# 66 slots instead of 68, quarter blocks, moved residuals and statistics, and inverse roots by Newton steps on VectorE

## The reference, cut to what matters

```
h = layernorm(x)                                # GNN: three layers
for i in range(3):
    m = h @ weight[i];  aggr = A^T @ m          # A = (adj != 0), per graph
    h = gru_cell(aggr, h)                       # sigmoid, sigmoid, tanh
x = x + h
xn = layernorm(x)                               # FFN: mixture of 8 experts
H = gelu(xn @ W1 + b1)                          # 128 -> 512
probs = softmax(H @ Wg + bg);  e = argmax(probs)
out = x + probs[e] * (H @ Wd[e] + bd[e])        # only the chosen expert counts
```

## Time and profile before

| | us |
|---|---|
| median of 3 runs (lowest, highest) | 468.53 (468.18, 469.12) |
| the profiled execution's own time | 469.11 |
| its span, first to last instruction | 467.4 |
| busy: PE, PEld (weight loads), DVE, ACT, POOL | 455.7, 377.4, 356.8, 323.0, 360.2 |
| indirect scatters to `sorted_rows` (line 580), busy | 63.9 in 64 instructions |
| indirect scatters to the output (line 591), busy | 35.6 in 36 and 31.8 in 32 |
| matmuls of the experts (line 858, 512 instructions) | 60.3 |

### The profile page before, as it was taken

One profiled execution on the slowest core, in us unless ns is written; L12 is line 12 of the kernel. 1 busy time (PEld: TensorE's weight loads), 2 busy tenths in 40 slices (PEclk: granted clock), 3 DMA queues, 4 the chain that ended last, 5 costly groups with the idle time before them and its releaser, 6 DMA issues.

```text
span 467.4 us, 10216 instructions
## 1 busy us (share of the span) xinstructions
PE 455.7 (97%) x3047; PEld 377.4 (81%) x3047; DVE 356.8 (76%) x1152; ACT 323.0 (69%) x576; POOL 360.2 (77%) x346
## 2 busy tenths in 40 slices
PE   8999999999999999999999999999999999999993
PEld 5777888888888888888888777777768989989993
DVE  5789878789888898887987889879778556556642
ACT  3776887777977769877788798888762553454340
POOL 4478997599978999889977757777777777277576
PEclk9999999999999999999999999999999999999998
DMA  7711455411234432111121111111452335454110
GB/s 199 211 42 51 137 145 148 136 45 45 58 86 109 132 100 80 52 45 47 51 58 51 52 47 40 59 53 58 134 142 79 112 115 167 126 155 118 38 52 28
DMA packets 69525, 42.10 MB, mean 90 GB/s; under 512 B 9548, under 2 KB 66128, under 8 KB 69472
## 3 DMA queue, kind: packets, MB, share of 16 engines
q1 hardware_dynamic: 64048, 32.33, 24.5%
q0 software_dynamic: 4224, 8.92, 5.5%
q10 hardware_dynamic: 1200, 0.20, 0.2%
HBM read 16.90 MB, written 9.84 MB: 57 GB/s over the span
## 4 chain that ended last, share of the span: by engine, by line
PE 90%; ACT 4%; DVE 3%; issue 1%; SPq 1%; POOL 1%; DMA 0%; POOLq 0%; DVEq 0%
PE bank L614 20%; PE bank L616 19%; PE bank L615 19%; PE bank L858 12%; PE bank L645 9%; PE bank L781 3%; ACT adj_i L1068 2%; PE bank L834 2%; PE bank L632 2%; PE bank L737 1%; PE bank L652 1%; PE bank L851 1%; SPq L372 1%; POOL out_dram L591 1%; DVE xrow L1277 0%
## 5 line engine op out<-in xcount | busy, mean ns | idle before, releaser
L1068 ACT ACTIVATE adj_i<-bank,b1c 128x512 f32<-128x512 f32 x132 | 88.6, 687 | 68.1 <-PE bank L616 67.4
L580 POOL DMA_INDIRECT sorted_rows<-xrow,pos x64 | 63.9, 999 | 24.4 <-issue 23.1
L477 POOL TENSOR_TENSOR diff<-hT,n_sb 128x512 f32<-128x512 f32 x48 | 67.3, 1403 | 17.4 <-ACT n_sb L955 17.3
L479 POOL TENSOR_TENSOR diff<-z_sb,diff 128x512 f32<-128x512 f32 x48 | 63.3, 1319 | 3.8
L858 PE MATMUL bank<-wd_sb,adj_i 128*128 x512 | 60.3, 275 | 0.0
L858 PEld LDWEIGHTS bank<-wd_sb,adj_i 128*128 128x128 f32 x512 | 59.0, 192 | 0.3
L614 PE MATMUL bank<-ag_hi,wf_hi 128*128 128x512 f32 x144 | 59.0, 410 | 0.1
L614 PE MATMUL bank<-hT_hi,w_hi 128*128 128x512 f32 x132 | 56.9, 431 | 1.1 <-ACT adj_i L1068 0.7
L615 PE MATMUL bank<-ag_lo,wf_hi 128*128 128x512 f32 x144 | 57.0, 396 | 0.0
L616 PE MATMUL bank<-ag_hi,wf_lo 128*128 128x512 f32 x144 | 56.9, 395 | 0.0
L614 PE MATMUL bank<-hT_hi,whh_hi 128*128 128x512 f32 x132 | 55.9, 424 | 0.0
(11 more groups left out here) (199 smaller groups left out, 1056.0 us busy)
## 6 DMA issues: line engine op xcount, KB each, us to landing
bands<-hT SPq DMA_DIRECT2D x192, 64.0 KB, 2.2
adj_i<-sorted_rows SPq DMA_DIRECT2D x64, 72.0 KB
xrow<-in_x_dram SPq DMA_DIRECT2D x16, 256.0 KB, 3.3
adj_i<-in_adj_dram SPq DMA_DIRECT2D x16, 256.0 KB, 3.8
wd_sb<-in_L_ffn_Wd_dram SPq DMA_DIRECT2D x8, 256.0 KB, 3.0
sorted_rows<-xrow,pos POOLq DMA_INDIRECT x64, 2.3
A<-wd_sb SPq DMA_DIRECT2D x4, 256.0 KB
hT<-wd_sb SPq DMA_DIRECT2D x4, 256.0 KB
```

The lines of the kernel that those rows point to most:

```text
L477: nc.gpsimd.tensor_tensor(diff[:, b, :], hT[:, g, :], n_sb[:, b, :], ALU.subtract).then_inc(diff_ok, 1)
L479: nc.gpsimd.tensor_tensor(diff[:, b, :], z_sb[:, g, :], diff[:, b, :], ALU.mult).then_inc(zd_ok, 1)
L580: nc.gpsimd.indirect_dma_start(out=sorted_rows, out_offset=bass.IndirectOffsetOnAxis(ap=pos[:, g, j:j + 1], axis=0), in_=xrow[:, g * GR + ...
L1068: nc.scalar.activation(HT[:, hb, k, 0:n], HB[k][:, 0:n], ACT.Gelu, bias=b1c[:, k:k + 1]).then_inc(done, 1)
```

## The change

The last six slots are now made of eight halves (four slots, all of slot group 15) and eight quarters of 32 rows (two slots, all of slot group 16). With quarters the worst case of padding is smaller, so SLOTS is 66. The number of slot groups stays 17. Sixteen copies of weights and biases take the place of eight. SP issues the first eight weight copies right behind `tab_ok` 2, before it waits for the scatters and before it loads slot group 6. The other eight and all biases go beside slot groups 6 to 13. The reads of table values lose their runtime bounds check.

The second table has three kinds of blocks, so `rest()` has more instructions and more stages that wait for each other.

In the gate, ScalarE takes `turned_high(1)` before the gelus of group 0 and does all four of these in a row. VectorE takes `turned_low(1)` earlier. The residual of the last unit moves to the end of gate step 4, and the last two groups' statistics from steps 4 and 5 to 5 and 6. The inverse roots of the last two groups are made on VectorE, by an integer first guess and three Newton steps, in gate steps 7 to 10. GpSimd's `pow` between the scatters goes.

TensorE waits for half of the gelus only, before the first two chunks of a slot group's hidden layer, and reads the table for slot group 0 ahead of them. `last_rows` has another order.

```diff
-    PIECE = P // 2
-    SLOTS = -(-((TOK + E * (PIECE - 1)) // PIECE) // PIECES)
+    HALF, QUARTER = P // 2, P // 4
+    HALVES = QUARTERS = E
+    COPIES = HALVES + QUARTERS
+    SLOTS = -(-((TOK + E * (QUARTER - 1)) // QUARTER) // (P // QUARTER))
-    WHOLE = (SGROUPS - 1) * GR
+    WHOLE = SLOTS - HALVES * HALF // P - QUARTERS * QUARTER // P
...
             _, found = nc.values_load_multi_w_load_instructions(row[0:1, at:at + count], engines=(engine,), min_val=0, max_val=top,
+                                                                skip_runtime_bounds_check_because="the table is bounded where it is made")
...
-        LATE_SCALES = 6
+        LATE_SCALES = 7
+        REFINED = 3
... (SP)
+            def load_weights(first, count):
+                at = entries(mybir.EngineType.SP, wd_tab, WHOLE + first, count, (E - 1) * KC * P)
+                for k in range(count):
+                    sp.dma_start(wd_last[first + k], wd_sb[:, bass.ds(at[k], KC * P)]).then_inc(e_wd, 16)
             sp.wait_ge(tab_ok, 2)
+            load_weights(0, HALVES)
             sp.wait_ge(g_late, (GROUPS - EARLY) * GR * 16)
             sp.wait_ge(pad_ok, (E + 1) * 16)
             for sg in range(EARLY_SG, SGROUPS):
                 load_rows(sg)
-                if sg == EARLY_SG + 2:
-                    last_at = (places(... wd_tab ...), places(... bd_tab ...))
-                if inside(sg - EARLY_SG - 2, GR * PIECES):
-                    load_last(sg - EARLY_SG - 2, *last_at)
+                if inside(sg - EARLY_SG, QUARTERS):
+                    load_weights(HALVES + sg - EARLY_SG, 1)
+                    load_biases((sg - EARLY_SG) * 2, 2)
... (GpSimd)
-                if s == LATE_SCALES + 1:
-                    which = slice(SCALED[LATE_BATCH] * GR, GROUPS * GR)
-                    pool.wait_ge(g_var_late, 1)
-                    nc.gpsimd.tensor_tensor(xrow[:, which, RSTD], xrow[:, which, RSTD],
-                                            half[...], ALU.pow).then_inc(g_rstd_late, 1)
... (TensorE)
             def rows_ready(sg):
-                hold(pe, e_h, sg * KC)
+                hold(pe, e_h, sg * KC - 2)
             def expert_pieces(sg, j, o):
                 for k in range(KC):
-                    for h in range(PIECES):
+                    for h in range(pieces(sg)):
             def step(s):
+                    if s == 1:
+                        at = weights_at(0)
                     rows_ready(s)
                     hidden(s % 2, (0, 1), e_w1)
-                    at = weights_at(s - 1)
+                    if s > 1:
+                        at = weights_at(s - 1)
+                    pe.wait_ge(e_h, s * KC)
                     hidden(s % 2, (2, 3), e_w1)
             def last_rows():
+                pe.wait_ge(e_h, two * KC)
+                pe.wait_ge(e_wd, 2 * COPIES * 16)
+                slot_alone(one, 0, None)
+                slot_alone(one, 1, None)
                 pe.wait_ge(e_xhi, two + 1)
                 pe.wait_ge(e_xlo, two + 1)
-                for j in range(GR):
-                    pe.wait_ge(e_h, one * KC + j + 1)
-                    hidden(two % 2, (j,), e_w1, cols(two))
-                    slot_alone(one, j, at_one)
+                hidden(two % 2, range(KC), e_w1, cols(two))
+                slot_alone(one, 2, None)
+                slot_alone(one, 3, None)
... (ScalarE, gate_step)
-                if s > 0 and inside(s + 1, GROUPS):
+                if inside(s + 1, GROUPS):
                     turned_high(s + 1)
-                    gelus(s % 2, s, (0, 1), g_w1, g_h)
+                    gelus(s % 2, s, (0, 1) if s else range(KC), g_w1, g_h)
                 if s == 0:
-                    turned_high(1)
                     new_state(UN - 1)
... (VectorE)
+            def late_guess():
                 dve.wait_ge(g_mv, GROUPS)
+                ts(late_var, late_var, EPS, None, ALU.add).then_inc(g_newton, 1)
+                ts(root_i[:], late_var.bitcast(i32), 1, None, ALU.arith_shift_right).then_inc(g_newton, 1)
+                ts(root_i[:], root_i[:], -1.0, float(0x5f3759df), ALU.mult, ALU.add).then_inc(g_newton, 1)
+            def late_refined(n):
+                tt(root_sq[:], root, root, ALU.mult).then_inc(g_newton, 1)
+                stt(root_sq[:], root_sq[:], -0.5, late_var, ALU.mult, ALU.mult).then_inc(g_newton, 1)
+                stt(late_var if n == REFINED else root, root_sq[:], 1.5, root, ALU.add, ALU.mult).then_inc(g_newton, 1)
+                if s == UN:
+                    turned_low(1)
-                turn, norm = inside(s + 1, GROUPS), ...
+                turn, norm = s > 0 and inside(s + 1, GROUPS), ...
-                measured = GROUPS - 6 + s
-                stat = s in (4, 5)
+                measured = GROUPS - 7 + s
+                stat = s in (5, 6)
                 if turn:
                     turned_low(s + 1)
+                if s == 4:
+                    state_rows(UN - 1)
+                    residual(UN - 1)
... (VectorE, rest: the added stages)
+                ts(until[:, 2 * E + 1:2 * E + 2], until[:, 2 * E:2 * E + 1], float(LATE_WHOLE + HALVES // 2), None, ALU.max)
+                dve.wait_ge(t_late, 16)
+                stt(until[:, 2 * E + 2:LISTS], many_cum[:, 2, :], 1.0 / 4, until[...], ALU.mult, ALU.add)
+                dve.wait_ge(t_late, 17)
```

More of the change, by code:

```diff
@@ L135, in build @@
         slot_i, slot = sb("slot_i", [P, 1], i32), sb("slot", [P, 1])
[L136 to L140, removed]
+        place, over, over_q = (sb(n, [P, 1]) for n in ("place", "over", "over_q"))
+        upward = sb("upward", [P, E])
+        ends_i, ends = sb("ends_i", [P, 3, E], i32), sb("ends", [P, 3, E])
+        many, many_cum = sb("many", [P, 3, E]), sb("many_cum", [P, 3, E])
+        many_t = sb("many_t", [P, 3, E, E])
         begins, offs = sb("begins", [P, LISTS + 1]), sb("offs", [P, LISTS + 1])
@@ L222, in places, with entries @@
         def places(engine, row, sg, top):
-            _, found = nc.values_load_multi_w_load_instructions(row[0:1, sg * GR:sg * GR + slots(sg) * pieces(sg)], engines=(engine,),
-                                                                min_val=0, max_val=top)
+            at, many_of = (first_piece(sg), slots(sg) * pieces(sg)) if pieces(sg) > 1 else (sg * GR, slots(sg))
+            return entries(engine, row, at, many_of, top)
+        def entries(engine, row, at, count, top):
+            _, found = nc.values_load_multi_w_load_instructions(row[0:1, at:at + count], engines=(engine,), min_val=0, max_val=top,
+                                                                skip_runtime_bounds_check_because="the table is bounded where it is made")
             return found
@@ L835, in turned_rows @@
                 last.then_inc(e_t, 1)
-            held = []
             def weights_at(sg):
@@ L1094, in gate_step @@
                         gate_rows(s + 3, 1)
-                if inside(s, GROUPS):
+                if s > 0 and inside(s, GROUPS):
                     gelus(s % 2, s, (2, 3), g_w1, g_h)
@@ L1541, in rest @@
+                stt(begins[:, E + 1:2 * E + 1], ends[:, 0, :], float(P), ecap[:], ALU.mult, ALU.add).then_inc(t_late, 1)
+                stt(begins[:, 2 * E + 2:LISTS], ends[:, 1, :], float(HALF), ecap[:], ALU.mult, ALU.add).then_inc(t_late, 1)
                 dve.wait_ge(t_late, 7)
+                tt(many_t[:], tri[:].unsqueeze(1).to_broadcast([P, 3, E, E]),
+                   many[:].unsqueeze(2).to_broadcast([P, 3, E, E]), ALU.mult).then_inc(t_late, 1)
+                dve.wait_ge(t_late, 10)
@@ L1560, in rest @@
+                dve.wait_ge(t_late, 24)
                 red(rsum[:], jump[:], AX.X, ALU.add).then_inc(t_late, 1)
+                tt(over[:], over[:], over_q[:], ALU.add).then_inc(t_late, 1)
+                dve.wait_ge(t_late, 26)
                 tt(esum[:], esum[:], over[:], ALU.add).then_inc(t_late, 1)
-                dve.wait_ge(t_late, 20)
+                stt(rsum[:], place[:], float(P), rsum[:], ALU.mult, ALU.add).then_inc(t_late, 1)
+                dve.wait_ge(t_late, 28)
                 ts(tab[:, 1:2], esum[:], float(E - 1), float(KC * P), ALU.min, ALU.mult).then_inc(t_made, 1)
@@ L1597, in step @@
                         dve.wait_ge(tab_ok, 2)
-                    if s == SGROUPS:
-                        dve.wait_ge(e_wd, 2 * GR * PIECES * 16)
-                        bias = [bd_last[:, j, :] for j in range(GR)]
+                    if pieces(s - 1) > 1:
+                        dve.wait_ge(e_wd, 2 * COPIES * 16)
+                        bias = [bd_last[:, (s - 1) * GR - WHOLE + j, :] for j in range(slots(s - 1))]
                     else:
@@ L1640, in _ @@
             gate_step(2)
-            gate_step(3)
-            state_rows(UN - 1)
-            residual(UN - 1)
-            for s in range(4, EARLY + 3):
+            for s in range(3, EARLY + 3):
                 gate_step(s)
```

125 lines of the change are left out of this document (67 added, 58 removed).

## The result

The changed kernel takes 464.82 us, the median of 6 runs (463.68 to 466.39); the kernel before took 469.03 in 6 runs beside it (468.18 to 469.35). The ratio is 0.9917, with a 95% interval of 0.9898 to 0.9937: faster by 3.9 us (the two medians differ by 4.2). The profiled execution took 465.0 with 463.3 of span, 4.1 less span than before.

A forecast was written before the change was run, and what follows sets the result against it. GpSimd's scatter queue was taken as the bound: -0.1 (opening) and -1.6 (pow), -2.6 (two scatters), +0.1 lost at slot group 14, -4.2 on its line; for the median, 468.53 - 4.15 = 464.4 us. The 8-in-10 range was 463.5 to 467.0.

The forecast's parts named there:

- the likeliest case's own range: Range of the median time if the main forecast, given 0.55, holds: 463.6 to 465.4 us.
- What bounds the kernel: GpSimd's scatter queue bounds the end; TensorE is 3.0 us ahead of mattering, narrowest at slot group 14, margin 1.6 less 0.1.
- The prediction's own sign of being wrong: GpSimd idle in the tail outside its drains; also a drain changed by over 1 us, or last product followed at once by last scatter.
- Two scatters, -2.6: GpSimd's last line: 68 slots become 66, so two scatters of 1.30 us each go, 2.6 us.
- The `pow`, -1.6: GpSimd between the gate's scatters: without the pow, all later scatters gain 1.6 us; VectorE's replacement costed at nothing.
- only the two scatters count: Rival, chance 0.15: the pow's 1.6 us do not arrive, through VectorE's new instructions or a late opening; -2.6, so 465.9 us.
- The opening: Gate's start: TensorE's waits for the low part go, gaining 0.5 us, bounds 0 and 1.4; ScalarE idles 0.4 us.
- The seam, 1.1: TensorE's waits of 0.75 for a gelu and 0.33 for register reads go: 1.1 us, bounds 0 and 1.1.
- The table, a stall of 0.9: Second table: more work in rest() takes about 1.0 us, so TensorE stalls 0.9 before transposing the table.
- Slot group 6, a stall of 0.5: Eight weight copies precede its row loads, first at 370.9; TensorE stalls 0.5 us, bounds 0 and 3.5.
- TensorE decides: Rival, chance 0.12: TensorE, busy 97%, sets the time; the sum is TensorE's alone, 3.6 us less, 464.9 us.
- TensorE's end, quarters like halves: TensorE's tail: two slots less save 3.4 us; a slot of quarters costs as one of halves, otherwise 1.8 us more.

The follow-up runs named there:

- Newton alone: The kernel before with only the pow replaced by Newton steps on VectorE (68 slots, old order, old seam): 468.50 us in 12 runs, 0.9998 of the kernel before.
- the old seam: The changed kernel with TensorE again waiting for all four gelus and reading the weight table between its halves: 464.86 us, 0.9926 of the kernel before.
- the second profile: The changed kernel profiled again, nothing altered; run again it took 464.91 us, 0.9925 of the kernel before.
- the lowered clock: Seven kernels, each the changed kernel with one or two edits, at a granted TensorE clock of 0.94 to 0.96: 527.52 to 536.80 us.
- the `pow` back: The changed kernel with the last two groups' inverse roots made by GpSimd's power again: 465.07 us, 0.9920 of the kernel before.

## Why the prediction was right, and where it was not

The time came out 0.4 us above the forecast, inside the likeliest case's own range; against the kernel before, 4.15 us were forecast and 3.9 measured. Point by point:

- **What bounds the kernel: failed in its reason.** "From its first scatter its queue never empties" and "the narrowest place is slot group 14", with "a margin of 1.6 less about 0.1 for the signal". The narrowest place is slot group 11, ahead of the second drain, with no margin. The rows of before give the reason. Slot group 6's first result starts at 396.20, so its scatter could have gone at 397.4; the first drain holds it until 405.58, 8.2 later. From there GpSimd takes 5.2 us for a slot group (four scatters) and TensorE 6.8, so GpSimd catches up 1.6 with each, and after five of them nothing of the 8.2 is left. The drain behind slot group 11 lets the results run ahead again, and so the tail in the earlier trace rows looks as if GpSimd had time in hand throughout. The prediction's own sign of being wrong, GpSimd idle outside its drains, stands there in the trace after. The signal was mis-sized too. VectorE's timeline after:

```profile
428.83 0.34 DVE L1665 SCALAR_TENSOR_TENSOR n_sb<-r_sb,adj_i 128x128 f32<-128x128 f32 x1
```

  The scatter that waited for it starts at 430.04, so 1.21 from the result's start and 0.87 from its end. It is the same 1.21 in the experiments with Newton alone, where the result starts at 429.89, and with the old seam (429.74). By it the margin at slot group 14 was 0.7 and not 1.5. The timeline of before had the sign already: one wait of 0.37 with a releaser on VectorE among gaps of 0.30.
- **Two scatters, -2.6: right** by the rows. 18 scatters from 438.12 to 460.11 stand (460.11 - 438.12) / 17 = 1.29 apart.
- **The `pow`, -1.6: right on GpSimd, wrong in the sum.** The 17th gate scatter starts at 302.35 in place of 305.19, the 16th at 301.08 in place of 302.34: 1.58 more. The wait of 1.47 at slot group 11 takes it back. The pairs with and without it differ at the last scatter by 0.3 (on the kernel before) and 0.4 to 0.7 (on the changed one). The rival that "only the two scatters count" named this outcome for the `pow`, with another mechanism.
- **What took its place: TensorE's earlier results, 0.9 to 1.2.** The sum gave TensorE 0.2. Its terms can be read from the starts of the same instruction before and after. All that lies ahead of the gate is 0.57 earlier in this execution, which is no merit of the change:

| the same instruction starts at | before | after | earlier by |
|---|---|---|---|
| transposes ahead of the gate's first hidden layer | 265.16 | 264.59 | 0.57 |
| a transpose of slot rows just ahead of the seam (line 834, then 852) | 341.81 | 340.10 | 1.71 |
| first expert products | 349.77 | 346.60 | 3.17 |
| the table's transpose | 360.52 | 358.36 | 2.16 |
| transposes of slot group 6's rows | 377.84 | 376.35 | 1.49 |
| slot group 11's first result (VectorE) | 430.27 | 428.83 | 1.44 |

  - The opening, "0.5, bounds 0 and 1.4": 1.14 (1.71 - 0.57). Neither wait of the earlier trace rows is left, which are 1.38, and 0.26 comes back in small pieces: TensorE is busy 26.88 of 27.00 from 264 to 291 and 38.86 of 39.00 from there to 330. The 0.4 of ScalarE came as foreseen (0.44 idle at 265.22), but no delay followed: `th` starts at 275.97, 0.57 earlier, as `z` did.
  - The seam, 1.1: 1.46. The waits that the profile lists are all gone (busy 14.09 of 14.09 us from 335.85 on, 13.02 before); by the starts they were longer than the idle times say, since the end of a TensorE instruction is modelled.
  - The table, a stall of 0.9: 1.01 (0.98 as listed).
  - Slot group 6, a stall of 0.5: 0.67 (0.55 as listed). The row loads start at 369.97 (forecast 370.9), the copies take 365.92 + 2.83 - 363.28 = 5.5 us for eight (forecast 5.0).
  - So -1.14 - 1.46 + 1.01 + 0.67 + 0.05 = -0.87 from the gate on; counted from the first scatter slot group 11's first result is 0.93 earlier (428.83 - 280.47 against 430.27 - 280.98). In the second profile, with stalls of 0.76 and 0.47, it is 1.23. The mis-sized terms are the opening, by 0.6, and the seam, by 0.4. So the rival "TensorE decides" holds up to slot group 11, and behind it GpSimd does, which the rival had not.

TensorE's timeline after, its two stalls:

```profile
358.36 0.82 PE L840 MATMUL bank<-ident,tab 128*1 128x128 f32 x6 [0.98 <-DVE tab L1622]
...
376.35 0.66 PE L852 MATMUL bank<-ident,xn 128*128 128x128 f32 x4 [0.55 <-DVE xn L1634]
```

SyncE's timeline after: the copies, and the row loads of slot group 6, each row for the issues of four transfers.

```profile
363.28 2.52 SPq L438 DMA_DIRECT2D A<-wd_sb  x4
365.92 2.83 SPq L438 DMA_DIRECT2D hT<-wd_sb  x4
369.97 3.10 SPq L431 DMA_DIRECT2D adj_i<-sorted_rows  x4
```

- **TensorE's end, quarters like halves: right.** TensorE's timeline: the last two slots of halves (128*64), the first slot of quarters (128*32), the start of the second:

```profile
451.97 1.97 PE L869 MATMUL bank<-hT,adj_i 128*64 128x128 f32 x32
453.87 1.08 PE L869 MATMUL bank<-z_sb,adj_i 128*32 128x128 f32 x32
454.77 0.28 PE L869 MATMUL bank<-bands,adj_i 128*32 128x128 f32 x2
```

  A slot of halves takes (453.87 - 451.97) / 2 = 0.95 us, a slot of quarters 454.77 - 453.87 = 0.90. From slot group 11's first result to the last result TensorE gained 2.9 where 3.4 were forecast; nothing waits for it, as the last result starts at 456.22 and its scatter at 460.11.

The two errors, -1.7 for GpSimd's line where nothing of it counted and -0.2 for TensorE where 0.9 came, nearly cancel: -1.7 + 0.1 against -0.93, and the earlier start of this execution gave 0.5 more. That the number fits so well is luck; only the term of the two scatters was right in size and in reason.

## What to carry to other kernels

A queue that drains somewhere can have its narrowest place just before a drain, if it is the faster one and catches up since the drain before (here 1.6 us with each slot group); look for the one small wait with a foreign releaser among the steady gaps, because from there on the other engine's time is the kernel's. A margin is read from when the signal arrives (here 1.21 us behind the result's start), not from when the result is done. An engine that is the last to run is not therefore the bound: a wait of 0.75 us put back on TensorE at the seam moved the last scatter by 0.8 to 1.1, 2.0 us given to GpSimd moved it by 0.3 at most. Before taking a drain out, ask what the end of the program will wait for.

## What the runs showed of the hardware

- A drain behind scatters costs by their number: 3.20 us of idle after 24, 8.19 after 88, and the stretch behind the last scatter's start grows from 3.2 to 4.7 between 18 and 42. It is not the time that counts: on the lowered clock the scatter behind the first drain starts 45 to 54 us later from the first scatter than in the changed kernel, and the idle behind them is 8.18 or 8.19 in all seven profiles.
- A small VectorE instruction can be caught by a scatter. Of three alike instructions in `rest()`, the first two take 0.17 us and the third 0.40. All three start within the scatter from 353.11 to 354.07; the third starts 0.54 us into it and ends with it:

```profile
353.50 0.17 DVE L1574 TENSOR_SCALAR ends_i<-ends_i 128x8 int32<-128x8 int32 x1
353.57 0.17 DVE L1575 TENSOR_SCALAR ends_i<-ends_i 128x8 int32<-128x8 int32 x1
353.65 0.40 DVE L1576 TENSOR_SCALAR ends_i<-ends_i 128x8 int32<-128x8 int32 x1
```

  What decides is where in the scatter the instruction starts. In the seven profiles at the full clock, of the small instructions with one input (CAST, TENSOR_SCALAR, COPY, 0.15 to 0.2 us usually) that start in a scatter's first 0.5 us, 2 of 188 took longer than usual; of those that start 0.5 to 0.7 us into it, 62 of 75, and nearly all of these end with the scatter. An instruction with two inputs in SBUF (SCALAR_TENSOR_TENSOR, 128x128) was never longer, 0 of 126 that start behind the first 0.52 us. Why is not shown.

  With the `pow` back, the scatters lie at another phase: the three start at 353.46 to 353.61, between two scatters, and take 0.17, `rest()` is done 0.43 earlier, and TensorE's stall for the table is 0.52 instead of 0.98. That, and slot group 6, for which TensorE did not wait there (0.55 less), is where the 0.9 us came from by which slot group 11's results were earlier.
